# Token loads by batch, cosine weights loaded without a wait, and projections in the order keys, queries, turns, values

## What is computed

```
x = x + _L0_xattn_ref(ctx_1024, ctx_1024, _layernorm(x, axis=-1), mask_Bx1xSxS2_ik1, ...)
x = x + _L0_ffn_ref(_layernorm(x, axis=-1), ...)
x = x + _L1_xattn_ref(_layernorm(x, axis=-1), ctx_1024, ctx_1024, ...)
x = x + _L1_ffn_ref(_layernorm(x, axis=-1), ...)
x = x + _L2_xattn_ref(_layernorm(x, axis=-1), ctx_1024, ctx_1024, ...)
x = x + _L2_ffn_ref(_layernorm(x, axis=-1), ...)
x = x + _L3_xattn_ref(_layernorm(x, axis=-1), ctx_1024, mask_Bx1x1xS2_ff0, ...)
x = x + _L3_ffn_ref(_layernorm(x, axis=-1), ...)
```

```
v = (value @ Wv.T + bv).reshape(n, -1, H, D)
k = (key @ Wk.T + bk).reshape(n, -1, H, D)
q = (query @ Wq.T + bq).reshape(n, -1, H, D)
```

## Time and profile before

| what | value |
| --- | --- |
| median of 3 runs | 4579.55 us (4572.97 to 4582.59) |
| time of the profiled execution | 4560.4 us |
| its span | 4558.6 us |
| PE, DVE, ACT, POOL busy over the span | 3880.8, 3103.2, 2059.7, 794.4 us |
| start to end of the projections of a0 | 0 to 137.4 us: PE busy 83.42, DVE 92.03, POOL 71.90 |
| entry and cosine sums of layer 1 | 1182.3 to 1330 us |
| token load and projections of a2 | 2869.0 to 2996.4 us: PE 82.31, DVE 91.03, POOL 37.10 |
| projections of a3 | 3743.0 to 3856.3 us: PE 83.57, DVE 90.36, POOL 37.11 |

### The profile page before, as it was taken

How to read it: one execution, slowest core, us unless ns; L and a number is a source line. 1 busy time by engine, 2 the same in 40 slices (tenths; PEclk the granted TensorE clock), 3 DMA queues, 4 the chain that set the end, 5 groups by cost and what they waited for, 6 DMA issues and landing times. The chain is left out here.

```text
span 4558.6 us, 83187 instructions
## 1 busy us (share of the span) xinstructions
PE 3880.8 (85%) x30525; PEld 2807.5 (62%) x30525; DVE 3103.2 (68%) x7110; ACT 2059.7 (45%) x3636; POOL 794.4 (17%) x510
## 2 busy tenths in 40 slices
PE   6699997799367999786389999579997987999899
PEld 5344444798265777676378888445555665455577
DVE  7666664446656666544556666678876888988688
ACT  3255554134013333243044444247775763777511
POOL 5424321401341000000023322310000003000000
PEclk9799998599678999898599999779998998999999
DMA  7333321201321000011054444532210005122000
GB/s 248 102 99 99 99 90 52 70 25 43 112 75 33 14 18 18 28 44 37 6 159 125 128 130 124 188 112 66 66 44 19 1 26 207 56 67 67 30 19 19
DMA packets 234365, 338.02 MB, mean 74 GB/s; under 512 B 39092, under 2 KB 132837, under 8 KB 234054
## 3 DMA queue, kind: packets, MB, share of 16 engines
q1 hardware_dynamic: 218168, 306.66, 21.1%
q0 software_dynamic: 15888, 27.23, 2.9%
HBM read 242.42 MB, written 107.01 MB: 77 GB/s over the span
## 5 line engine op out<-in xcount | busy, mean ns | idle before, releaser
L1905 ACT ACTIVATE a_pT<-a_psS 128x512 f32<-128x512 f32 x1536 | 835.9, 598 | 380.4 <-PE a_psS L1791 375.0
L1977 DVE TENSOR_REDUCE a_mx<-a_psA 128x1 f32<-128x512 f32 x1024 | 656.4, 685 | 77.4 <-PE a_psA L1769 77.4
L1806 PE MATMUL a_psZ<-a_pT,a_V 128*17 128x128 f32 x12288 | 485.8, 277 | 0.0
L1769 PE MATMUL a_psA<-a_ks,a_qs 48*128 48x512 f32 (+1 forms) x1536 | 402.8, 520 | 85.1 <-DVE a_mx L1977 36.8
L1973 DVE CUSTOM_DVE_ANT_0 a_scored<-a_psA,a_hide_q 128x512 bf16<-128x512 f32 x512 | 332.6, 688 | 182.1 <-PE a_psA L1769 181.0
L1806 PEld LDWEIGHTS a_psZ<-a_pT,a_V 128*17 128x17 f32 x12288 | 272.0, 97 | 269.4 <-issue 152.4
L1769 PEld LDWEIGHTS a_psA<-a_ks,a_qs 48*128 48x128 f32 (+1 forms) x1536 | 150.9, 191 | 331.4 <-DVE a_mx L1977 124.8
L1791 PE MATMUL a_psS<-a_qs,a_ks 50*128 50x512 f32 (+1 forms) x1536 | 316.3, 405 | 2.7 <-ACT a_pT L1905 0.8
L3245 DVE SCALAR_TENSOR_TENSOR ex_h<-ex_psU,ex_ub,ex_sg 128x512 f32<-128x512 f32 x129 | 96.9, 751 | 189.4 <-PE ex_psU L159 182.3
L1989 POOL TENSOR_TENSOR X<-X,a_osb 128x512 f32<-128x512 f32 x48 | 61.1, 1278 | 931.3 <-ACT a_osb L1892 913.3
L3191 ACT CAST ex_w_h<-X 128x1024 fp32r<-128x1024 f32 x102 | 106.0, 1040 | 151.0 <-DMA X<-in_L_ffn_gw 147.2
(11 more groups left out here) (606 smaller groups left out, 10221.8 us busy)
## 6 DMA issues: line engine op xcount, KB each, us to landing
a_qs<-a_q_parts SPq DMA_DIRECT2D x576, 64.0 KB, 2.3
a_ks<-a_k_parts SPq DMA_DIRECT2D x576, 64.0 KB, 2.3
a_k_parts<-a_p_kp SPq DMA_DIRECT2D x96, 256.0 KB, 2.6
a_q_parts<-a_p_qp SPq DMA_DIRECT2D x96, 256.0 KB, 3.1
X<-in_L_ffn_gw SPq DMA_DIRECT2D x36, 512.0 KB, 4.5
X<-in_L_ffn_up_w SPq DMA_DIRECT2D x36, 512.0 KB, 3.3
X<-in_L_ffn_down_w SPq DMA_DIRECT2D x36, 512.0 KB, 3.9
top_rows<-blank_rows SPq DMA_DIRECT2D x32, 514.0 KB, 5.0
```

The costliest lines, as they stand in the source:

```text
L1769: nc.tensor.matmul(psA[:, unit(a, par) % 3], qs[r, g % ring, p % 2, q * P:(q + 1) * P], ks[r, g % ring, p % 2], start=True, stop=True).the ...
L1806: last = nc.tensor.matmul(psZ[q * VP:q * VP + VW, g % 2, j * P:(j + 1) * P], V[:, b, kt, g % NG * GH + j, :], pT[:, p % 2, par, kt, q * P: ...
L1905: nc.scalar.activation(pT[:, p % 2, par, kt, :], psS[:, unit(t, par) % 3], ACT.Exp).then_inc(exp_done, 1)
L1977: nc.vector.tensor_reduce(mx[:, p // 2 % 2, par, p % 2, q:q + 1], psA[:, unit(a, par) % 3], AX_X, ALU.max).then_inc(a_used, 1)
```

## The change

- The 8 token loads leave the first block of the program, and the 4096 KB load leaves the end of `expert_choice`. `resident_projections` issues them itself, a batch at a time (`tokens`): batch 0 ahead of everything, batch 1 behind the second context, batch b+2 at the start of batch b. In a3 nothing is loaded.
- `cosine_attention` waits for no weights on entry. All five loads are issued behind the first context load of `cosine_sums`; POOL waits for the two vectors before its loop, SP for the rest at the end.
- The projections of a batch: PE does `K`, `Q`, the turn of batch b+1, `V`. DVE takes the values out after the low part of the turned tokens. ACT casts the context of b+1 behind the high part of the keys. The query weights are loaded and split ahead of the value weights.

```
-                for b in range(B):
-                    sp.dma_start(G.X[:, b * TB:(b + 1) * TB, :], x_dram[:, b * TB:(b + 1) * TB, :]).then_inc(x_loaded[b], 16)
...
-        load_weights(nc, [(G.X[:], x_dram.rearrange("(n p) d -> p n d", p=P))], back)
+    G.x_from = x_dram.rearrange("(n p) d -> p n d", p=P)
...
+                def tokens(b):
+                    if x_from is not None:
+                        tiles = slice(b * TB, (b + 1) * TB)
+                        sp.dma_start(G.X[:, tiles, :], x_from[:, tiles, :]).then_inc(G.x_loaded[b], 16)
+
...
+                tokens(0)
                 sp.dma_start(raw["wk"][:], rows(w.Wk)).then_inc(w_loaded["wk"], 16)
                 context(0)
+                sp.dma_start(raw["wq"][:], rows(w.Wq)).then_inc(w_loaded["wq"], 16)
                 sp.dma_start(raw["wv"][:], rows(w.Wv)).then_inc(w_loaded["wv"], 16)
-                sp.dma_start(raw["wq"][:], rows(w.Wq)).then_inc(w_loaded["wq"], 16)
                 context(1)
+                tokens(1)
...
                     if b + 2 < B:
+                        tokens(b + 2)
                         sp.wait_ge(cT_low, b + 1)
                         context(b + 2)
...
                     project(psK, "wk", lambda k: (cT_h[:, u, k, :], cT_l[:, u, k, :])).then_inc(k_in_psum, 1)
+                    pe.wait_ge(f.low_ready, b + 1)
                     if b == 0:
                         pe.wait_ge(w_low, 2)
+                    else:
+                        pe.wait_ge(q_low, b)
+                    project(psQ, "wq", lambda k: f.parts(0, k)).then_inc(q_in_psum, 1)
+                    if b + 1 < B:
+                        f.tensor_turn(pe, b + 1)
+                    if b == 0:
+                        pe.wait_ge(w_low, 3)
                     else:
                         pe.wait_ge(v_taken, b)
...
                     if b + 1 < B:
                         f.scalar_roots(act, b + 1)
+                    high_part(k_in_psum, psK, kp, bk, k_stored, k_high, b)
+                    if b + 1 < B:
                         context_high(b + 1)
-                    high_part(k_in_psum, psK, kp, bk, k_stored, k_high, b)
                     high_part(q_in_psum, psQ, qp, bqs, q_stored, q_high, b)
...
                     low_part(psK, kp, bk, k_high, k_low, b)
+                    low_part(psQ, qp, bqs, q_high, q_low, b)
+                    if b + 1 < B:
+                        f.vector_low(dve, b + 1, 0)
                     dve.wait_ge(v_in_psum, b + 1)
...
-        load_weights(nc, [(lng[:], bcast_row(A["L1_xattn_ln_g"])), (lnb[:], bcast_row(A["L1_xattn_ln_b"]))], loaded)
...
                 load(0, 0)
+                for tile, src in ((lng, "L1_xattn_ln_g"), (lnb, "L1_xattn_ln_b")):
+                    sp.dma_start(tile[:], bcast_row(A[src])).then_inc(loaded, 16)
+                for tile, src in later_loads:
+                    sp.dma_start(tile, src).then_inc(later_loaded, 16)
```

More of the change, by code:

```diff
@@ L1378, in resident_projections @@
         rows = lambda x: x.rearrange("(k p) d -> p k d", p=P)
+        x_from, G.x_from = G.x_from, None
+        G.x_loads += x_from is not None
         with nc.Block() as block:
@@ L1444, in _ @@
                     last.then_inc(v_in_psum, 1)
-                    pe.wait_ge(f.low_ready, b + 1)
-                    if b == 0:
-                        pe.wait_ge(w_low, 3)
-                    else:
-                        pe.wait_ge(q_low, b)
-                    project(psQ, "wq", lambda k: f.parts(0, k)).then_inc(q_in_psum, 1)
-                    if b + 1 < B:
-                        f.tensor_turn(pe, b + 1)
             @block.scalar
@@ L1476, in _ @@
                 f.scalar_high(act, 0, 0)
+                weight_high("wq")
                 weight_high("wv")
-                weight_high("wq")
                 act.wait_ge(scaled, 1)
@@ L1509, in low_part @@
                     last.then_inc(done, 1)
-                dve.wait_ge(G.x_loaded[0], 16)
+                dve.wait_ge(G.x_loaded[0], 16 * G.x_loads)
                 f.vector_norm(dve, 0, 0, first=True)
@@ L1514, in _ @@
                 f.vector_low(dve, 0, 0)
-                weight_low("wv", 1)
-                weight_low("wq", 2)
+                weight_low("wq", 1)
+                weight_low("wv", 2)
                 dve.wait_ge(small_loaded, 16 * 5)
@@ L1523, in _ @@
                     if b + 1 < B:
-                        dve.wait_ge(G.x_loaded[b + 1], 16)
+                        dve.wait_ge(G.x_loaded[b + 1], 16 * G.x_loads)
                         f.vector_norm(dve, b + 1, b + 1)
                     low_part(psK, kp, bk, k_high, k_low, b)
+                    low_part(psQ, qp, bqs, q_high, q_low, b)
+                    if b + 1 < B:
+                        f.vector_low(dve, b + 1, 0)
                     dve.wait_ge(v_in_psum, b + 1)
@@ L2059, in cosine_attention, with cosine_sums @@
         loaded = sem("loaded")
-        load_weights(nc, [(win[:], A["L1_xattn_w_in"].rearrange("(k p) o -> p k o", p=P)),
-                          (wout[:], A["L1_xattn_w_out"].rearrange("(h p) d -> p h d", p=P)),
-                          (bout[:], bcast_row(A["L1_xattn_b_out"]))], loaded)
-        cosine_sums(nc, A, G, z_dram, gsum)
+        loads = [(win[:], A["L1_xattn_w_in"].rearrange("(k p) o -> p k o", p=P)),
+                 (wout[:], A["L1_xattn_w_out"].rearrange("(h p) d -> p h d", p=P)),
+                 (bout[:], bcast_row(A["L1_xattn_b_out"]))]
+        cosine_sums(nc, A, G, z_dram, gsum, loads, loaded)
         cosine_weights(nc, A, G, win, gsum, coef, wwh)
         cosine_apply(nc, A, G, z_dram, win, wout, bout, coef, wwh)
-def cosine_sums(nc, A, G, z_dram, gsum):
+def cosine_sums(nc, A, G, z_dram, gsum, later_loads, later_loaded):
     with ExitStack() as ctx:
@@ L2125, in _ @@
                     sp.wait_ge(cx_loaded[n], (B // 2 + 1 - n) * 16)
+                sp.wait_ge(loaded, 32)
+                sp.wait_ge(later_loaded, 16 * len(later_loads))
             @block.tensor
@@ L2178, in step @@
                         nc.gpsimd.tensor_tensor(z[:, u], z[:, u], o, ALU.add).then_inc(done, 1)
+                pool.wait_ge(loaded, 32)
                 rounds(pool, step)
@@ L2710, in expert_choice @@
         run_experts(nc, A, G, rows_dram[0:N_TOK, :], x_dram, index)
-    with ExitStack() as ctx:
-        back = ctx.enter_context(stage_semaphores(nc, "l1f_"))("back")
-        load_weights(nc, [(G.X[:], x_dram.rearrange("(n p) d -> p n d", p=P))], back)
+    G.x_from = x_dram.rearrange("(n p) d -> p n d", p=P)
 def shared_expert(nc, A, G, rows_dram, sT_dram, x_dram):
@@ L3302, in build_program @@
         G.x_loaded, G.out = x_loaded, out_dram
+        G.x_from, G.x_loads = x_dram, 0
         G.blank_rows = nc.dram_tensor("blank_rows", [P, TOP1_ROW], F32).ap()
```

3 lines of the change are left out of this document (removed).

## The result

| | before | after |
| --- | --- | --- |
| median | 4576.69 us (4572.97 to 4582.59, 4 runs) | 4524.49 us (4521.86 to 4529.04, 4 runs) |
| profiled execution, and its span | 4560.4, 4558.6 us | 4529.04, 4527.3 us |

The ratio is 0.9888, with a 95% interval of 0.9874 to 0.9902: 52 us less. A second comparison gave 4525.46 against 4572.02, 0.9901 (0.9885 to 0.9916), 47 us less. The forecast was 47.9 us.

A forecast was written before the change was run, and what follows sets the result against it. Bounds: waits at three starts, DVE's 10.89 us steady batch, SP's queue ending a2 and a3, a0's masks. Cosine 13.7, a0 12.7, a2 16.7, a3 4.8 sum to 47.9, so 4579.55 becomes 4531.6 us (4517 to 4552).

The forecast's parts named there:

- first batches: Projections, batches 0 to 2: the new order gains 0.9 us despite POOL's memsets, between -2 and 3.
- inside of a batch: Projections: the low part of the queries no longer waits for the values, 1.1 us sooner.
- Cosine entry: Start of the cosine stage: both waits ahead of the first context load go, 13.7 us (12 to 14.3).
- Tokens in a2: Start of a2: loading by batch brings keys 12.9 us sooner (11 to 14), less 1.0 for a later load.
- Tokens in a0: Start of a0: projections start near 5.0, first keys at 16.1 against 23.36, 7.2 us (5 to 8.5).
- Steady batch: Projections: undisturbed `xn`, PE becomes the longer engine, 9.5 us per batch instead of 10.9, 1.4 less.
- The rival that moves the stop to the keys: Projections: POOL's subtraction stops the key step instead of `xn`; gain 40, time 4539, chance 0.08.
- The values at the low clock: Rival, projections: PE runs values at 1.2 GHz, period near 12.3; gain 28, time 4552, chance 0.10.
- Order in a3: a3 up to the query store of batch 4: 0.9 + 2 batches of 1.4 + 1.1 = 4.8 us (1 to 8).
- Order in a2: a2 up to the query store of batch 4: the new order gives 4.8 us of the 16.7 there.
- a0: Whole a0: 7.2 from the start, 1.8 and 4.0 from the order, less 0.3, 12.7 us (9 to 16).
- The ends of a2 and a3: SP issues back to back for 34.0 us in a2, similarly in a3; the queue, not an engine, sets the end.

The follow-up runs named there:

- tokens only: Kernel before with the tokens loaded by batch and nothing else changed; 4558.42 us, ratio 0.9968.
- changed again: Changed kernel without any edit, for a second profile and second times; 4525.46 us, ratio 0.9901.
- no tokens: The group later kernel with the tokens loaded as before the change, all batches at entry; 4504.03 us.
- group later: Changed kernel with two a0 mask loads a batch earlier, GpSimd's stack memsets over four batches, third group's loads moved into the following attention; 4488.35 us, 0.9815.
- Cast first: Changed kernel with ScalarE casting the next context ahead of the keys' high parts again; 4543.97 us, ratio 0.9931.
- cast alone: Kernel before with only ScalarE's cast of the next context moved behind the keys' high parts; 4569.97 us, ratio 0.9994.
- Settings spread: Changed kernel with GpSimd's memsets of the query and key stacks as one piece in each of batches 0 to 3; 4507.58 us.
- order only: Kernel before with only the new order of projections, casts, low parts and query and value weight loads; 4558.54 us, ratio 0.9969.

## Why the profile pair shows 31 us and the runs show 52

Between the two profiles the places gained 10.6 + 14.0 + 16.6 + 6.1 = 47.3 us, and stretches that no edit touches lost 16.0: the attention of a2 5.4 (752.0 against 746.6), the shared expert 5.7, the last stage 5.2, and small amounts of both signs elsewhere.

The shared expert, from its first weight load to the first load of the choice of tokens: 230.8 to 231.5 us in nine profiles, 236.5 in the first one of the changed kernel, 243.2 to 243.4 in four. The changed kernel itself had 236.5 once and 231.5 in its second profile, so this is not a matter of code. The whole of that stage in tokens only, changed, changed again; in a row stand the stretch, its length, busy time and instructions of PE, its weight loads, DVE, ACT and POOL, the granted clock, and DMA:

```profile
1904.40:2147.60 243.20, 195.64 (x1064) 170.22 (x1064) 99.89 (x211) 93.12 (x130) 0.00 (x0) 0.84 0.15 46
```
```profile
1888.80:2125.30 236.50, 190.65 (x1064) 164.54 (x1064) 99.88 (x211) 93.12 (x130) 0.00 (x0) 0.87 0.15 47
```
```profile
1886.70:2118.10 231.40, 187.34 (x1064) 161.20 (x1064) 99.87 (x211) 93.12 (x130) 0.00 (x0) 0.88 0.15 48
```

The work is the same, 1064 matmuls and the same busy time of VectorE and ScalarE. The granted clock is 0.84, 0.87 and 0.88, and PE is busy for 195.6, 190.7 and 187.3 us: the share of the time at 1.2 instead of 2.4 GHz differs. The Trainium skill, in "TensorE: Matmul & The Clock Gate", section "Part 1: The HAM clock gate", says that the gate samples the engine's activity on a clock of its own, which does not restart with the kernel. By that rule one kernel can get several values for one stage, and the two profiles of the changed kernel did; that the rule is what makes these values, no row shows.

The last stage took 262.2 to 262.7 us, at a granted clock of 0.94, in four profiles, all of kernels that load tokens as before and reach it at 4294 to 4297, and 265.8 to 271.5, at 0.92 to 0.90, in the ten others, among them no tokens. The token loads are not the cause, or not the only one. Whether it is the moment at which the stage begins, or chance, stays open: the tokens-only kernel reached it at 4292.2 and took 267.7.

The profile of the kernel before has the low value in both, and its time is 12 and 13 us below the medians of 17 and 28 of its runs (4572.0 and 4573.5); the first profile of the changed kernel has a higher one in both, and is 4 and 5 us above its medians. The difference of these two single profiles was off by 15 to 21 us over the whole, while the entry of the cosine stage repeats within 1 us over all the kernels that share it.

## Why the prediction was right, and where its steps were off

The time, 4531.6 foretold and 4524.5 measured, lies inside the range, and the sum of the terms, 47.9, is between the two measured differences. The main mechanisms are shown: the waits at the three starts, and the place of the cast. That the sum came so close is in part luck, since terms were off in both directions: the first batches cost where a gain was foretold, the inside of a batch gave four times its term, and the start of a2 in the profile of the kernel before was itself 1.3 us longer than in the others with the one large load. Term by term:

- *Cosine entry*, 13.7: 13.4 to 14.3 in the places of ten profiles, 13.9 in time. That fits with the 0.6 us taken off for the five loads, and without.
- *Tokens in a2*, 12.9 less 1.0: the first keys come 13.3 us sooner behind the first load than in the profile of the kernel before, and 11.6 to 12.0 sooner than in the four others with the one large load. Alone the place was 12.5 shorter, and 10.2 where the rest is shorter. The charge for later loads is borne out: from the first keys to the end, a2 is 0.8 longer in tokens only than before, and 1.4 longer with the group later than in no tokens. It has a row, too: VectorE waited 2.93 us for the tokens of batch 7, issued at 2925.70 behind the 12 loads of the first group.
- *Tokens in a0*, 7.2: 7.9 to 8.5 at the first keys, 6.0 and 6.7 at the end of the projections, 8.4 and 4.7 at the feed-forward stage. The block began at 4.09, not 5.0.
- *Steady batch*, 9.5: 9.3, with TensorE as the bound and VectorE waiting 0.30. Cast first and cast alone show that it is the place of ScalarE's cast that frees `xn`, as the step said.
- *The rival that moves the stop to the keys* is excluded: two key pieces take 1.40 under the subtraction. They read PSUM first, then a bias and a high part in SBUF. The Trainium skill, "SBUF — State Buffer", section "Who interferes with whom", counts a VectorE instruction as stopped if it has two SBUF inputs; this form, with one of the two a column of biases, is not of them in the trace. Its other rule, that the first of a TENSOR_SCALAR in a two-port mode and a GpSimd instruction blocks the other wholly, fits `xn` and the 4.04 us above.
- *The values at the low clock* did not come. A window over three batches of a2 and one over five of a3 show PE busy throughout at the full clock. In the first two batches the granted clock is lower, 0.75 from 2859.5 to 2873 and 0.87 from 2873 to 2887; there GpSimd's rows set the pace, as said below.

```profile
2902.00:2930.00 28.00, 28.00 (x170) 24.66 (x169) 23.23 (x51) 12.57 (x20) 7.21 (x3) 1.00 0.84 288
3752.00:3799.00 47.00, 47.00 (x284) 41.33 (x283) 40.95 (x93) 23.16 (x37) 12.03 (x5) 1.00 0.75 258
```

- *First batches*, a gain of 0.9 over batches 0 to 2, between -2 and 3: here the step had the sign wrong. They cost. From the first subtraction to the fourth a3 took 36.2 us before (3749.6 to 3785.8) and 37.4 after (3717.1 to 3754.5), a loss of 1.2, though the third of these batches is 0.9 shorter; in a2 the loss is 1.7 and, in the second profile, 2.3. In a0 the batches 1 and 2 take 12.1 us in place of 11.0. Behind GpSimd's long piece stands a ring: its end releases the input of the root, then root, keys' high parts, cast, subtraction, and the next long piece. The cast's later place makes it 1.2 us longer, as the idle time of GpSimd between the first long piece and the next subtraction in a3 shows: kernel before, changed, cast first, cast alone.

```profile
3762.24 2.45 POOL L1493 TENSOR_TENSOR a_p_cT_l<-a_p_cT,a_p_cT_h 128x1024 fp32r<-128x1024 f32 x1 [1.42 <-ACT a_p_cT_h L1460]
3730.89 2.38 POOL L1506 TENSOR_TENSOR a_p_cT_l<-a_p_cT,a_p_cT_h 128x1024 fp32r<-128x1024 f32 x1 [2.57 <-ACT a_p_cT_h L1472]
3746.02 2.42 POOL L1506 TENSOR_TENSOR a_p_cT_l<-a_p_cT,a_p_cT_h 128x1024 fp32r<-128x1024 f32 x1 [1.42 <-ACT a_p_cT_h L1472]
3766.34 2.35 POOL L1494 TENSOR_TENSOR a_p_cT_l<-a_p_cT,a_p_cT_h 128x1024 fp32r<-128x1024 f32 x1 [2.57 <-ACT a_p_cT_h L1460]
```

  The wait is long with the cast behind the keys' high parts and short with the cast ahead of them, whatever the order of the products. Settings spread fits: with the piece cut in two the ring takes 2.4 + 4.4 + 2.5 = 9.3 us, no more than TensorE's batch.
- *Order in a3*, 4.8: 6.1. From the first keys to the start of SP's unbroken stretch it gained 64.7 - 59.0 = 5.7: a loss of 1.2 over the first three batches; 3.8 in batches 3 and 4, where 2.8 was foretold and batch 3 of the kernel before took 11.5; and 4.4, where 1.1 was foretold, because the queries' low parts of batch 4 begin 0.6 us behind the start of GpSimd's subtraction in place of 5.0. The step counted the 1.1 of the values and left out the 2.1 of `xn` in that batch and the 1.3 by which the subtraction itself is later. Of these 7.0, 1.3 is lost where SP is still busy with the stores of the keys. The first keys come 1.0 earlier, which nothing in the sum foretells and no run explains, and SP's stretch is 0.7 longer.
- *Order in a2*, 4.8: 5.5 up to SP's stretch; order only gives 5.1 from the first keys to the end, and the changed kernel 4.1 over tokens only.
- *a0*, 12.7 in all: 10.6 in the first pair, where keys gave 8.4. Batches up to 5 gave back 2.3, mostly through that ring, the two waits for masks then gave 4.5, where 4.0 was foretold. By the feed-forward stage the two profiles of the changed kernel stand 10.6 and 15.5 ahead. Of the 1.8 + 4.0 foretold for the order, 2.2 are there in the first pair, and the start, 1.2 larger than foretold, covered part of the rest; what the order is worth in a0 stays open, as order only shows 1.1, the changed kernel ends 4.6 and 6.6 ahead of tokens only, and the same code there differs by 5.
- *The ends of a2 and a3*: SP's stretch is the bound of the projections as said, now 36.6 and 36.0 us in place of 34.0 and 35.3. Group later shows it by taking issues out.

## What to carry to other kernels

When an engine's step is stopped by another engine, move the release of the other one past it, and then look at the longest piece in that other engine's queue: the same delay enters the ring that runs through it. A start that waits for whole transfers is worth what its rows say, here to one or two microseconds, because nothing else runs there. At the end of a block whose queue issues back to back, take transfers out of the block, and look whether the next block gives the time back; putting the same data into fewer issues gained nothing here.

## What the runs showed of the hardware that was not expected

- One program's stage took 231.5 and 236.5 us in two executions, and up to 243.4 in kernels with the same code there, at granted clocks over the stage of 0.88, 0.87 and 0.84.
- VectorE steps on four numbers per partition, 0.17 us long elsewhere, took 2.42 and 4.04 us and ended with a memset on GpSimd, which only writes.
- Two stores of keys, of double size, were issued in 0.89 us where four took 1.80; the queries right behind them took 2.16 where four took 2.63, the stretch of 35 us became 0.8 shorter, and the next block began 5.9 in place of 4.4 us behind its end.
